# Router and expert kernel: 3 KB weight runs for two experts, later splits, and a product that reads its rows in the target's order

## The reference

```
w = weights[conditions]                        # 32 of 200 matrices, 128 x 128
y = einsum('bct,bcd->bdt', x, w)               # "condition product", 4096 rows of 1024
probs = softmax(y @ gate_w.T)                  # 64 experts
w, sel = top_k(probs, 8); w = w / sum(w)       # 8 experts a row
# each expert takes its first 256 rows (CAP) in order
h = silu(inp @ wg) * (inp @ wu)                # 1024 -> 384
out = h @ wd                                   # 384 -> 1024
x = x + scatter-add of out, weighted           # then the second layer: base and LoRA product with its own router
```

## Time and profile before

| what | value |
|---|---|
| runs, median (lowest to highest) | 2384.96 us (2383.49 to 2385.33) |
| the profiled execution | 2386.41 us |
| its span, first to last instruction | 2384.7 us |
| mean granted clock of PE | 0.996 |
| PE busy | 2353.6 us (99%) |
| DVE, ACT, POOL busy | 1663.2, 1368.0, 1397.3 us |
| chain that ended last | PE 95%, DMA 1%, DVE 1%, ACT 1%, issue 1% |
| of it L686, the condition product | 2% |

### The profile page before, as it was taken

One profiled execution on the slowest core, in us unless ns is written; L12 is line 12 of the kernel. 1 busy time (PEld: TensorE's weight loads), 2 busy tenths in 40 slices (PEclk: granted clock), 3 DMA queues, 4 the chain that ended last, 5 costly groups with the idle time before them and its releaser, 6 DMA issues.

```text
span 2384.7 us, 35342 instructions
## 1 busy us (share of the span) xinstructions
PE 2353.6 (99%) x12783; PEld 2074.9 (87%) x12783; DVE 1663.2 (70%) x2876; ACT 1368.0 (57%) x2251; POOL 1397.3 (59%) x1023
## 2 busy tenths in 40 slices
PE   8988999999999999999999999999999999999999
PEld 5677888888888888888888888888889999999999
DVE  6887888887878888888888788888862244444443
ACT  5766776776767777777777677777761211111110
POOL 4035778777778777877777777777710122222222
PEclk9999999999999999999999999999999999999999
DMA  9999989899998998988989989899866354444441
GB/s 347 389 325 272 284 287 281 274 283 288 281 291 278 289 279 279 284 283 279 286 276 286 281 276 282 278 291 280 273 196 132 86 140 130 130 130 129 129 121 60
DMA packets 251664, 582.20 MB, mean 244 GB/s; under 512 B 82553, under 2 KB 108538, under 8 KB 251490
## 3 DMA queue, kind: packets, MB, share of 16 engines
q1 hardware_dynamic: 184674, 401.18, 51.2%
q0 software_dynamic: 55424, 159.89, 25.9%
q10 hardware_dynamic: 11392, 18.88, 2.2%
HBM read 456.38 MB, written 123.45 MB: 243 GB/s over the span
## 4 chain that ended last, share of the span: by engine, by line
PE 95%; DMA 1%; DVE 1%; ACT 1%; issue 1%; ACTq 0%; SPq 0%; DVEq 0%
PE ps L822 26%; PE ps L839 22%; PE ps L938 17%; PE ps L821 13%; PE ps L896 5%; PE ps L818 4%; PE ps L686 2%; PE ps L931 2%; PE ps L819 2%; PE ps L696 1%; PE ps L911 1%; DMA raw<-in_L_ffn_wg 1%; PE ps L709 0%; PE ps L708 0%; DMA bmR<-accd 0%
## 5 line engine op out<-in xcount | busy, mean ns | idle before, releaser
L822 PE MATMUL ps<-XX,HR 128*128 128x512 f32 x2688 | 959.8, 396 | 0.0
L821 PE MATMUL ps<-XX,LR 128*128 128x256 f32 x2688 | 750.4, 279 | 0.0
L590 POOL DMA_INDIRECT Xg<-yd,idx x496 | 637.8, 1286 | 153.5 <-issue 150.8
L1527 DVE TENSOR_TENSOR LR<-raw,HR 128x1536 fp32r<-128x1536 f32 x384 | 657.4, 1751 | 14.8 <-ACT HR L1093 14.7
L822 PEld LDWEIGHTS ps<-XX,HR 128*128 128x128 f32 x2688 | 505.2, 188 | 104.2
L1093 ACT ACTIVATE HR<-raw 128x1536 fp32r<-128x1536 f32 x384 | 556.6, 1478 | 22.0 <-DMA raw<-in_L_ffn_wd 9.8
L821 PEld LDWEIGHTS ps<-XX,LR 128*128 128x128 f32 x2688 | 507.5, 189 | 17.6
L612 POOL DMA_INDIRECT accd<-ot,toki x128 | 254.1, 1985 | 167.2 <-ACT ot L1147 147.7
L938 PE MATMUL ps<-MH,xT 128*128 128x392 f32 x1536 | 335.8, 344 | 0.0
L839 PE MATMUL ps<-HR,hH 128*128 128x512 f32 x768 | 300.1, 391 | 6.9 <-DVE hL L1574 6.9
L839 PE MATMUL ps<-LR,hH 128*128 128x512 f32 x768 | 303.5, 395 | 0.0
(11 more groups left out here) (217 smaller groups left out, 3224.5 us busy)
## 6 DMA issues: line engine op xcount, KB each, us to landing
raw<-in_L_ffn_wd SPq DMA_DIRECT2D x128, 768.0 KB, 4.6
raw<-in_L_ffn_wg SPq DMA_DIRECT2D x124, 768.0 KB, 7.2
raw<-in_L_ffn_wu SPq DMA_DIRECT2D x124, 768.0 KB, 7.0
yd<-yrow ACTq DMA_DIRECT2D x32, 512.0 KB, 7.2
x<-accd SPq DMA_DIRECT2D x32, 512.0 KB, 5.1
out<-osb SPq DMA_DIRECT2D x31, 512.0 KB, 3.0
xt<-in_x SPq DMA_DIRECT2D x25, 512.0 KB, 7.7
accd<-xt SPq DMA_DIRECT2D x25, 512.0 KB, 5.1
```

The costliest lines, as they stand in the source:

```text
L590: eng.indirect_dma_start(Xg[:, c, q, :], None, yd4, bass.IndirectOffsetOnAxis(ap=idx4[:, e % 4, i:i + 1], axis=0))\
L821: eng.matmul(bank(out, 0, CAP), wl, xx[:, 0:CAP], start=False, stop=False)
L822: mm = eng.matmul(bank(out), wh, xx, start=False, stop=(k == 7))
L1527: eng.tensor_tensor(LR[:, (n + 2) % NHL, :], raw[:, n % NRAW, :], HR[:, (n + 2) % NHL, :].bitcast(F32), ALU.subtract).then_inc(s_L, 1)
```

## The change

1. `condition(i)` reads x at a step. With t = (f a j h), 4 x 32 x 4 x 2, half h takes the positions (f j a) of that h: neighbouring elements of the moving operand lie 8 elements (32 bytes) apart. The result in PSUM is already in the target's order, and `evac_y` and `evac_q` copy runs of 128 elements, bank 0 to the even 128-blocks of `yrow` and bank 1 to the odd ones.
2. The order of a row in yd becomes (f h j a). `turn`, `turn_rows`, the gate's copy (L1344, reads contiguous, writes at a step of two elements) and the block number in `up` follow.
3. The units of wg and wu of experts 0 and 1 are read in runs of two rows, 3072 bytes instead of 1536: unit A has f = 0, 1 and unit B f = 2, 3. Still four DMAs a unit.
4. On SP the two stores of KEPT[0] move from before unit 4 (and behind its wait for the gathered rows of experts 0 and 1) to behind unit 3; the five of KEPT[1] from behind unit 5 to behind unit 4.
5. ACT: `spread(2)` goes behind the four `high_0(0)`; `split("gA", 1)` behind `high_h(2)`. DVE: `index(2)` behind `low_0(0)`; `product(1)` ahead of `split("dB", 0)`; `join(2)` and `product(2)` earlier, with `count(3)` between them and `token(3)` behind; expert 1's splits gA to uB behind `low_h(2)`, and the two `column` copies behind these.

```diff
                 if parted(n):
-                    v = (wg if k[0] == "g" else wu)[e].rearrange("(f a h j) i -> h j a f i", f=4, a=32, h=2)
-                    d = raw[:, n % NRAW, :].rearrange("p (f i) -> p f i", f=4)
+                    v = (wg if k[0] == "g" else wu)[e].rearrange("(f a j h) i -> j a f (h i)", f=4, a=32, j=4)
+                    f0 = 0 if k[1] == "A" else 2
+                    d = raw[:, n % NRAW, :].rearrange("p (f s) -> p f s", f=2)
                     for j in range(4):
-                        eng.dma_start(d[32 * j:32 * j + 32], v[0 if k[1] == "A" else 1, j]).then_inc(d_raw[n % NRAW], 16)
+                        eng.dma_start(d[32 * j:32 * j + 32], v[j, :, f0:f0 + 2]).then_inc(d_raw[n % NRAW], 16)
...
                     for c in range(2):
                         eng.wait_ge(d_xr[c], 16)
+                load_unit(n)
+                if n == NRAW - 1:
                     for k in KEPT[0]:
                         store_kept(k, d_ak[0])
-                load_unit(n)
-                if n == NRAW + 1:
+                if n == NRAW:
                     for k in KEPT[1]:
                         store_kept(k, d_ak[1])
...
-                    eng.matmul(bank(h), wall[:, i % 16, :], xin(i)[:, h * 512:(h + 1) * 512],
+                    eng.matmul(bank(h), wall[:, i % 16, :], xin(i).rearrange("c (f a j h) -> c h f j a", f=4, a=32, j=4)[:, h],
...
-                        k = 4 * f + q
+                        k = 2 * q + f
...
-                        i = 2 * (k % 4) + k // 4
-                        mm = eng.transpose(bank(4 + 2 * c + k // 4, (k % 4) * P, (k % 4 + 1) * P), v[:, i * P:(i + 1) * P], ident[:, :])
+                        mm = eng.transpose(bank(4 + 2 * c + k // 4, (k % 4) * P, (k % 4 + 1) * P), v[:, k * P:(k + 1) * P], ident[:, :])
...
+            def block(e, k):
+                return k if e < 2 else 4 * (k % 2) + k // 2
...
-                eng.activation(yrow[:, i % NY, 0:512].rearrange("q (f j a) -> q f a j", f=2, j=8),
-                               bank(0).rearrange("q (f a j) -> q f a j", f=2, j=8), ACT.Copy).then_inc(s_yr, 1)
+                eng.activation(yrow[:, i % NY, :].rearrange("q (f h s) -> q h f s", f=4, h=2)[:, 0],
+                               bank(0).rearrange("q (f s) -> q f s", f=4), ACT.Copy).then_inc(s_yr, 1)
...
-            spread(2)
             for g in range(2):
                 for c in range(2):
                     high_0(0, g, c)
+            spread(2)
...
-            split("gA", 1)
             copy_2(2)
             silu(2)
             high_h(2)
-            for k in ("gB", "uA", "uB", "dA"):
+            for k in ("gA", "gB", "uA", "uB", "dA"):
                 split(k, 1)
...
-            index(2)
             for g in range(2):
                 for c in range(2):
                     low_0(0, g, c)
+            index(2)
...
+            product(1)
             split("dB", 0)
-            product(1)
             low_h(1)
+            join(2)
             count(3)
-            split("gA", 1)
+            product(2)
             token(3)
-            join(2)
-            product(2)
             low_h(2)
+            for k in ("gA", "gB", "uA", "uB"):
+                split(k, 1)
             column(0)
             column(1)
-            for k in ("gB", "uA", "uB", "dA"):
-                split(k, 1)
+            split("dA", 1)
```

More of the change, by code:

```diff
@@ L815, in up @@
                             s, o = (u + 2) % NHL, (k % 4) * I + b * P
-                            wh, wl, xx = HR[:, s, o:o + P], LR[:, s, o:o + P], XX[:, e % 2, k, :]
+                            wh, wl, xx = HR[:, s, o:o + P], LR[:, s, o:o + P], XX[:, e % 2, block(e, k), :]
                             if k == 0:
@@ L1343, in _ @@
             for f in range(4):
-                mm = eng.tensor_copy(gwp.rearrange("e (f j a) -> e f j a", f=4, j=8)[:, f],
-                                     gw.rearrange("e (f a j) -> e f j a", f=4, j=8)[:, f])
+                mm = eng.tensor_copy(gwp.rearrange("e (h f j a) -> e f a j h", h=2, f=4, j=4)[:, f],
+                                     gw.rearrange("e (f a j h) -> e f a j h", f=4, j=4, h=2)[:, f])
             mm.then_inc(s_gwp, 1)
@@ L1367, in evac_q @@
                 eng.wait_ge(s_Y, 2 * i + 2)
-                eng.tensor_copy(yrow[:, i % NY, 512:D].rearrange("q (f j a) -> q f a j", f=2, j=8),
-                                bank(1).rearrange("q (f a j) -> q f a j", f=2, j=8)).then_inc(s_yq, 1)
+                eng.tensor_copy(yrow[:, i % NY, :].rearrange("q (f h s) -> q h f s", f=4, h=2)[:, 1],
+                                bank(1).rearrange("q (f s) -> q f s", f=4)).then_inc(s_yq, 1)
             def low_y(i, f):
```

## The result

The changed kernel takes 2438.98 us (median of four runs, 2438.28 to 2440.69) against 2385.14 us for the kernel before: ratio 1.0222, 95% interval 1.021 to 1.0235, 53.8 us slower. The forecast was 2432.

What follows compares the result with a forecast made beforehand. PE's own work was taken to bound the kernel, plus about 31 us of standing still. 2386.4 + 58 - 3 - 1 - 6.5 = 2433.9, less 1.45 gives 2432 us; own range 2421 to 2444, with rivals 2374 to 2444.

Steps and rivals of the forecast that it cites:

- +58 us for 128 instructions: Routing stage: the strided product costs +0.473 us on 120 PE instructions and +0.156 on eight, +58 us.
- booked 4: Routing stage: plain copies close the 0.3 us gaps of pairs, -3 us; last tile and less crowded DMA queues, -1 us.
- 1.79 ns for a lonely element: Condition product in the routing stage: estimated price of each strided element, making an instruction 916 ns instead of 443.
- twice the price if each pass fetches for itself: Rival, routing stage: product fetches every element once per pass (or PE's clock drops), 2490 to 2550 us; chance 0.06.
- DVE's read in the earlier trace: Rival, condition product: only DVE's strided-read price shows, 0.34 ns an element, +22 us, 2397 us in all; chance 0.10.
- The third term: Start of the experts: expert 1's splits moved behind block 2 remove PE's stall, -6.5 us, between -10 and -2.
- The two-row runs: Weight loads of experts 0 and 1: 3072-byte packets flow at 337 GB/s, each unit costing 2.3 instead of 3.5 us.
- The five stores ahead of dB: Expert 0: KEPT[1] stores delay dB to about 177.5 to 178.5 and the down product by 0 to 1.7 us, 1 taken.
- my fourth rival: Start of experts: dB or gA holds PE as long, third term about 0, 2439 us; decides only if dB lands after 184.
- the first terms: Routing stage: strided product +58 us, copies -3 us, last tile and DMA queues -1 us.
- The join of block 3: Expert 1: block 2 waits for this join as ACT's chain is late by 0 to 5 us; 2.8 taken.
- The piece with the moved spread: Before expert 0: moving spread brings the XX copies forward, -0.6 us.

Runs made afterwards that it cites:

- fp32r_step: Kernel before, with the high part of the logits product (256 fp32r columns) reading its moving operand at a 32-byte step; 2407.6 against 2397.0 us, single run.
- splits_only: Kernel before with only ACT's and DVE's order changed (expert 1's splits behind block 2, spread, index and count moved); 2397.17 against 2396.96 us, ratio 1.0002.
- after_kept: Changed kernel with the five KEPT[1] stores behind unit dB of expert 0 again; 2442.86 us, ratio 1.0191 against the kernel before.
- two_copies_sp: Changed kernel with a contiguous product read, two permuting copies a half and the seven kept stores in their old places; 2397.52 us, ratio 1.0000 against the kernel before.
- before_ports: Kernel before, with wg and wu units of experts 0 and 1 loaded by four DMAs over 128 partitions instead of 32; 2423.75 against 2386.49 us, ratio 1.0158.

## Why the prediction was right, and where it was not

**The place and the size were right.** I said that the routing stage is bound by PE, so that the product's own cost is paid in full: +58 us for 128 instructions. Measured: 0.927 - 0.443 = 0.484 for 120 of them and +1.6 for the first eight (7.71 instead of 6.08 us), 59.7 us. The rest of the stage shrank by 6.1 us, where I had booked 4: 5.0 up to the last product, which is the 0.3 us of waiting in a pair, and 1.1 behind it. The stage grew by 53.6 us.

**The price behind the 58 was right by luck.** I took 1.79 ns for a lonely element, from strided writes of ACT and DVE and a strided weight load, backed by PE's own pace for 16 neighbouring bytes, and assumed one fetch of each element. fp32r_step shows lonely elements 0.84 ns apart, so the 1.79 ns are not the price of one, and for an fp32r operand my estimate would have been too high by a factor of two. That fp32 came out at 1.81 ns has another reason, most likely two fetches of 0.9. Then my rival "twice the price if each pass fetches for itself" had its premise right and its price wrong. The nearest row was that of DVE's read in the earlier trace rows, which I had put among the rivals: its +0.34 ns an element stands beside +0.38 measured for fp32r. For the fp32 product it would have given only +22 us.

**The third term was wrong: -6.5 forecast, about -1.3 measured** (-0.6, -2.4 and +1.6 in the table). Its parts:
- The wait of 6.93 us went, as said, and the freed 8.6 us are seen in splits_only. But I read the weight stream as a thing that would be just in time. It was what set the start of expert 1: in splits_only, with ACT's idle wait removed, PE waits for gA, gB, uA and uB one by one.
- The two-row runs were booked to flow at 337 GB/s, by packet size. They flow at 223. The comparison with 383 GB/s in the earlier trace rows was one of whole rows over 128 partitions against parts over 32, and I put all of the difference on the packet.
- The five stores ahead of dB were priced at 0 to 1.7 us, 1 taken. dB landed 19.2 us after expert 0's first matmul, where I had forecast 15 to 16, and PE's first down product began 24.6 us after it (20.2 before): 4.4 us, and 2.6 more by slow matmuls. after_kept, with these stores back in their place, was no faster at this point (25.8 us), so it is not shown that the stores alone are the cause. This was my fourth rival, "the stall isn't gone but turned", and its 2439 us is what was measured; I had left it without a chance of its own. Its condition did not hold, though: dB landing after 184 would be 21.8 us after expert 0's first matmul. It hit the number also because the first terms together were nearly right (+53.6 against +54).
- The join of block 3, on which block 2 of expert 1 waits, was priced at 2.8 us. The wait was there, 1.10 us:

```profile
264.09 0.50 PE L822 MATMUL ps<-XX,HR 128*128 128x512 f32 x1 [1.10 <-DVE gu L1567]
```

- The piece with the moved spread became 0.6 us shorter, as said. That is no clear result, since two_copies_sp, which has the move too, takes 14.70 us for it, as the kernel before does (14.62).

The forecast's main line held because the term whose size was right is nine times as large as the one that was wrong.

## What to carry to other kernels

A permutation is not free because it is an access pattern. Given to the engine that bounds the stage it is paid in full, and the copies that it makes plain are cheap on engines that had time. If PE must read at a step, keep two fp32 in 16 bytes (+5% here) and let the copy do the rest; here that was no gain over a plain read, only no loss. Before an unneeded wait is moved out of the way, ask for the next resource behind it: here the stream of weights was late by nearly as much as the wait was long, and the freed 8.6 us came back as four smaller waits. And a price borrowed from other engines should be tried on the engine in question, once at each data type: three rows agreed on 1.8 ns, and fp32r_step shows that PE's price for one lonely element is half of that.

## What the runs showed of the hardware that I had not expected

- PE's moving operand, 512 fp32 columns in one instruction: 0.443 us contiguous, 0.464 at 8 bytes, 0.908 at 16, 0.927 at 32. With 256 fp32r columns: 0.117 contiguous, 0.21 at 32 bytes. The Trainium skill (SBUF — State Buffer, Door 1: The DMA port swizzle) says that two hits in a 16-byte line are needed, and that agrees: 0.464 us with two fp32 a line, 0.908 with one. It also calls a step of four fp32 free, and there the measurement differs: at 16 bytes nearly all of the price is there.
- DMAs whose source has an outermost dimension of 4 moved 94 GB/s in a window of before_ports, at a DMA share of 0.27; DMAs over 32 partitions moved 223 to 227, at a share of 1.05 to 1.09, in windows of the kernels before and after.
- A step of 32 bytes costs fp32 0.95 ns more a column (0.484 us for 512) and fp32r 0.38 (0.097 us for 256, from a single run).
